# Fewer moving columns in the up products of experts with 129 to 224 tokens, in a fused attention and mixture-of-experts block

## The reference

```python
x = x + jnp.tanh(g_xattn[0]) * _L0_xattn_ref(_layernorm(x, axis=-1), ctx_512, ctx_512)
x = x + jnp.tanh(g_ffn[0]) * _L0_ffn_ref(_layernorm(x, axis=-1), L0_ffn_w_cls, L0_ffn_bias, L0_ffn_w_gate_up, L0_ffn_w_down)
```

```python
buf = jnp.zeros((E, CAP, H), xf.dtype).at[ids_s, pos].set(x_exp[order], mode='drop')
gu = jnp.einsum('ech,ehf->ecf', buf, w_gate_up)
g, u = jnp.split(gu, 2, axis=-1)
act = jax.nn.silu(g) * u
y = jnp.einsum('eci,eih->ech', act, w_down)
```

## Time and profile before

| | us |
|---|---|
| median of 3 runs | 2288.61 |
| lowest, highest | 2286.43, 2290.40 |
| the profiled execution, its own time | 2303.04 |
| its span, first to last instruction | 2301.2 |
| PE busy in the span | 2114.8 (92%) |
| DVE busy | 1453.7 (63%) |
| ACT busy | 1245.7 (54%) |
| POOL busy | 1072.1 (47%) |

### The profile page before, as it was taken

How to read it: one execution, slowest core, us unless ns; L and a number is a source line. 1 busy time by engine, 2 the same in 40 slices (tenths; PEclk the granted TensorE clock), 3 DMA queues, 4 the chain that set the end, 5 groups by cost and what they waited for, 6 DMA issues and landing times.

```text
span 2301.2 us, 48610 instructions
## 1 busy us (share of the span) xinstructions
PE 2114.8 (92%) x14776; PEld 1228.3 (53%) x14777; DVE 1453.7 (63%) x2463; ACT 1245.7 (54%) x1833; POOL 1072.1 (47%) x1241
## 2 busy tenths in 40 slices
PE   5999999989998596899999999999999999999996
PEld 2555554445554344456556564744656766454464
DVE  6788888888887564346446572833564865462383
ACT  3787777666775436235445463632553764353364
POOL 3127888877887465224322441622342643241262
PEclk9999999999999797999999999999999999999998
DMA  5567666657564656457666593955585986665582
GB/s 148 144 176 179 169 186 156 177 154 189 159 152 120 217 149 163 150 156 215 180 187 185 172 281 83 302 161 160 161 259 133 286 235 173 188 174 162 150 250 47
DMA packets 569277, 407.81 MB, mean 177 GB/s; under 512 B 213558, under 2 KB 489142, under 8 KB 569200
## 3 DMA queue, kind: packets, MB, share of 16 engines
q1 hardware_dynamic: 506112, 334.10, 50.1%
q0 software_dynamic: 46336, 72.10, 13.2%
q10 hardware_dynamic: 16752, 0.65, 0.5%
HBM read 319.33 MB, written 103.16 MB: 184 GB/s over the span
## 4 chain that ended last, share of the span: by engine, by line
PE 66%; DVE 14%; issue 9%; ACT 3%; POOL 3%; another core or an unknown queue 2%; DMA 1%; SPq 1%; DVEq 0%; POOLq 0%; ACTq 0%
PE psum L1673 35%; PE psum L1703 16%; DVE mx L1159 5%; PE psum L1560 5%; PE psum L1532 3%; PE psum L1545 2%; PE psum L1613 2%; DVE xgt L1328 1%; DVE stats L1124 1%; PE psum L1573 1%; DVE wgu L1316 1%; PE psum L1584 1%; DMA out_dram<-ys,slots 1%; PE psum L1509 1%
## 5 line engine op out<-in xcount | busy, mean ns | idle before, releaser
L1673 PE MATMUL psum<-xgt,wgu 128*128 128x256 f16 (+3 forms) x6336 | 907.0, 301 | 40.3 <-issue 25.1
L1673 PEld LDWEIGHTS psum<-xgt,wgu 128*128 (+1 forms) x6336 | 573.8, 98 | 372.7 <-issue 54.8
L807 POOL TENSOR_TENSOR spare<-spare 128x1 f32<-128x1 f32 x164 | 141.9, 865 | 856.1 <-PE psum L1703 432.5
L1703 PE MATMUL psum<-wdn,apair 128*128 128x512 f16 x1968 | 458.6, 384 | 19.1 <-issue 14.2
L1159 DVE TENSOR_REDUCE mx<-psum 128x2 f32<-128x512 f32 x512 | 327.3, 683 | 84.0 <-PE psum L1532 71.9
L1316 DVE SCALAR_TENSOR_TENSOR wgu<-wraw,wgu 128x1024 f16<-128x1024 f32 x264 | 318.4, 1216 | 41.2 <-ACT wgu L940 37.4
L724 POOL DMA_INDIRECT lists<-entry,dest x256 | 268.4, 1049 | 114.3 <-issue 69.7
L923 ACT ACTIVATE prob<-psum 128x512 f32<-128x512 f32 x512 | 277.3, 598 | 72.1 <-PE psum L1545 38.6
L1338 DVE SCALAR_TENSOR_TENSOR a<-psum,sg 128x512 f32<-128x512 f32 x132 | 91.0, 689 | 350.2 <-PE psum L1673 335.9
L1328 DVE COPY xgt<-psum 128x1024 f16<-128x1024 f16 x256 | 167.0, 682 | 225.0 <-PE psum L1613 206.4
L1703 PEld LDWEIGHTS psum<-wdn,apair 128*128 128x128 f16 x1968 | 187.9, 99 | 223.7 <-issue 30.4
(11 more groups left out here) (157 smaller groups left out, 1943.5 us busy)
## 6 DMA issues: line engine op xcount, KB each, us to landing
wraw<-in_L_ffn_w_gate_up_dram SPq DMA_DIRECT2D x264, 512.0 KB
wraw<-in_L_ffn_w_down_dram SPq DMA_DIRECT2D x132, 512.0 KB
x<-in_x_dram SPq DMA_DIRECT2D x16, 1024.0 KB
xr<-in_x_dram SPq DMA_DIRECT2D x16, 1024.0 KB
out_dram<-x SPq DMA_DIRECT2D x16, 1024.0 KB
pairs<-xs SPq DMA_DIRECT2D x16, 1024.0 KB
qs<-qh SPq DMA_DIRECT2D x248, 64.0 KB
qs<-ql SPq DMA_DIRECT2D x128, 64.0 KB
```

The source lines that it names most:

```text
L1673: mm = pe.matmul(ps_gu[:, s, h, 0:nt * P], w[:, a, k, :], xgt[:, c, k, 0:nt * P], start=(k == 0 and (a, c) == (0, 0)), stop=(k == KB - 1 a ...
L1703: mm = pe.matmul(psum[:, Y_BANK[i] + n2, :], apair[:, o, k, c * P:(c + 1) * P], w[:, a, k, :], start=(k == 0 and (a, o) == (0, 0)), stop=( ...
```

## The change

The width of the up products is taken from a table. It is unchanged for the arms 1, 3 and 4. In arm 2 the up products stream 224 columns where they streamed 256. The test that leads into arms 1 and 2 is now for at most 224 tokens where it was 256, so that an expert with 225 to 256 tokens goes into arm 3 (384 columns and three blocks). The down products, the transposes, and all that the other engines do are as they were. On TensorE no instruction is added, taken away or moved; the moving operand and the output of the 192 up matmuls of arm 2 are 32 columns narrower, and one constant of a comparison differs.

```diff
@@ -41,6 +41,7 @@
 TOPK = 8
 CAP = 512
 CT = CAP // P
+UP_COLUMNS = {1: P, 2: 7 * P // 4, 3: 3 * P, 4: CAP}
 FF = 512
 FB = FF // P
 ROUTE_SCALE = 1.5
@@ -1670,7 +1671,7 @@
                 pe.wait_ge(wgu_lo, 2 * n + h + 1)
                 for k in range(KB):
                     for a, c in TERMS:
-                        mm = pe.matmul(ps_gu[:, s, h, 0:nt * P], w[:, a, k, :], xgt[:, c, k, 0:nt * P],
+                        mm = pe.matmul(ps_gu[:, s, h, 0:UP_COLUMNS[nt]], w[:, a, k, :], xgt[:, c, k, 0:UP_COLUMNS[nt]],
                                        start=(k == 0 and (a, c) == (0, 0)), stop=(k == KB - 1 and a == 1))
                 mm.then_inc(gu_full, 1)
 
@@ -1774,7 +1775,7 @@
             def step2(e, last):
 
                 n = pe.value_load(filled[0:1, bass.ds(e, 1)], min_val=0, max_val=ntok)
-                with pe.If(n < 2 * P + 1):
+                with pe.If(n < UP_COLUMNS[2] + 1):
                     with pe.If(n < P + 1):
                         body(e, 1)
                     with pe.Else():
```

## The result

| | before | changed |
|---|---|---|
| median, us (4 runs each) | 2288.44 | 2264.49 |
| lowest, highest | 2286.43, 2290.40 | 2263.25, 2268.57 |
| the profiled execution | 2303.04 | 2268.57 |
| its span | 2301.2 | 2266.8 |

The ratio is 0.9902, with a 95% interval from 0.989 to 0.9914: 24.0 us faster, 1.0%. The forecast was 2268.3, or 20.3 us.

A forecast was written before the change was run, and what follows sets the result against it. TensorE was taken to bound the 33 steps; nine arm 2 steps of 2.19 us and one of 0.57 gave 20.3 us, taken off the median 2288.61 for 2268.3 us, range 2262 to 2275.

The forecast's parts named there:

- TensorE bounds the 33 steps: Whole step loop: TensorE's waits add up to 29 us over 1300 us, so a microsecond less there shortens the total.
- The price of 32 columns, 2.56 us a step: Up products of arm 2: 0.417 ns a column, 13.35 ns a matmul, 25.6 us over ten steps if nothing else holds TensorE.
- the one for paired loads: Skill's rule for matmuls each with its own weight load: 0.13 ns a column, winning only 8 us over 1920 up matmuls.
- The sequencer costs nothing at 224: Up products of arm 2: sequencer needs about 18.6 us against 18.40 streaming, covered by a lead of at least 1.4 us.
- A new wait of 0.37 us for `dn_lo(1)`: Before arm 2's first down matmul: low down weights on VectorE come late, so a step gains 2.19 us, not 2.56.
- The step from 1340.11 gains only 0.57: One arm 2 step where VectorE started late after a 1.85 us wait: down product at 20.39 us, gain only 0.57.
- the first rival: Start of arm 2's down products: the VectorE to TensorE latency hides, all 25.6 us come through, 2263.0 us; chance 0.12.
- The step from the profiled execution to the median: Whole kernel: profiled execution lies 14.4 us above the median; the 20.3 us are taken off the median, 2288.61.
- No expert changes arms: Branch into arm 2: its ten experts have at most 206 tokens, the nearest above 258, so the cost is nothing.
- the rival: Branch of `step2`: two or more experts fall into arm 3, a loss of 13.3 us and more, 2301.9; chance 0.03.

The follow-up runs named there:

- the split kernel: 224 columns as in the change, with the wait for the second low part of the down weights moved 9 down matmuls later; 2261.2 us, ratio 0.9884 to before.

## Why the prediction was right, and where not

- *TensorE bounds the 33 steps.* Right. What the steps of arm 2 lost on TensorE went out of the total, and no other engine came due, down to 192 columns.
- *The price of 32 columns, 2.56 us a step.* Right. The paces measured are 82.5 and 89.2 ns (192 and 208 columns, with the loop written out), 95.8 (224, from 18.40 us in the split kernel), 102.5 (240), 109.2 (256), 152.6 (360) and 162.6 (384), 0.417 ns a column throughout. The rule N/2.4 + 2.5 ns, which the prediction took from the Trainium skill (TensorE: Matmul & The Clock Gate, section Back-to-back issue gap), gives each of them to 0.1 ns; the one for paired loads does not hold here between 192 and 384 columns.
- *The sequencer costs nothing at 224.* Right, with less to spare than it looked: at 208 it costs 0.3 us inside the up products, and at 192, once the wait is split, all that the narrower width would bring.
- *A new wait of 0.37 us for `dn_lo(1)`.* Right in kind and place, and shown by taking it away. Its size was 0.27 to 0.31 us, since the way from VectorE to TensorE took 0.23 to 0.28 us in arm 2 and not the 0.34 read in arm 1. That row holds a different path, through `closing`, with a check or two more. Most of this way is not the signal: in the step shown, TensorE's check of `wdn_lo` (line 1712) begins 0.04 us after `dn_lo(1)` ends, and the other 0.2 us go by in register instructions and further checks before the first down matmul. Worth 0.7 us in all.
- *The step from 1340.11 gains only 0.57.* Wrong. The stop of 1.85 us on VectorE did not come again: that step gained 2.29 like the others. Nor did VectorE run "without a gap" after it; it stood still for 0.97 us ahead of `act_lo` of j=1, waiting for ScalarE. A stop seen once, from outside the engines, need not come again in its step. Worth 1.7 us.
- *The last step* gained 2.6 us rather than 2.19, because it does not wait for `dn_lo(1)` at all: its up products run 0.29 us over streaming in both traces, and `dn_lo(1)` is ready by then. Worth 0.4 us. With these three terms 20.3 becomes 23.1, and 24.0 were measured; the 0.9 between them is inside the interval.
- *The total.* That the stretch lost 20.3 us, the figure of the whole forecast, is chance: for its nine steps the forecast had 18.1 (eight of 2.19 and one of 0.57). By the total alone the first rival, no new wait and 2263.0 us, is nearer to the 2264.5 measured than the forecast's 2268.3. What decides for the forecast's mechanism is the trace, and the run with the split wait.
- *The step from the profiled execution to the median.* The 20.3 us were taken off the median, so that nothing hung on the 14.4 us by which the profiled execution was longer. That was the right way: for the changed kernel this excess was 4.1 us. That of before lay largely in steps 0 and 1 (132.8 us against 122.7), which vary.
- *No expert changes arms.* Right. The price of one, 15.4 us, left out the two transposes in `opening`; it is 16.7 against the 256 columns, 19.0 against the 224. With two such experts the kernel is slower than before, as the rival said, by 15.5 us where it gave 13.3.

## What to carry to other kernels

Where a matrix engine streams without idle time, its columns have a fixed price (here 0.417 ns each), and padding to a round number of blocks can be dropped to the width that the data need, as long as no group falls into the next wider arm. Before pricing it, look at the next thing to be late: here VectorE's low parts and TensorE's own sequencer stood within a microsecond of the up products. The first came just due at 240 columns, where `dn_lo(1)` ends the 0.28 us ahead that the way to TensorE takes; at 224 it took back about 0.3 of the 2.56 us. And read a variable kernel by the stretch that does not vary: steps 2 to 30 repeat to a tenth of a microsecond while whole executions scatter by several.

## What the runs showed of the hardware

- At 192 columns, with a weight load for each matmul and register arithmetic for the weights' address, the second half of the up products took 8.91 us for 96 matmuls, about 92 ns each. Inside each run of 24 it was 86 ns; the rest stood at the changes from one run to the next. With fixed addresses and the loop written out all 192 ran at 82.5 ns (15.84 us).
- From the end of a VectorE instruction to the matmul that waited for it passed 0.23 to 0.28 us where register instructions and further checks stood between (the steps in the loop). Where the wait stood on the weight load itself, in the last step of the changed kernel, that load began 0.05 us after the end (2244.62 after 2244.57), and it did so in the last step with 208 columns too.
- The profile's name for a wait on a line with several semaphores can be plainly wrong: 0.25 us were put down to `wdn` in a kernel where the part waited for had been ready for 4 us.
- Writing out a loop of two rounds, at 208 columns, made each of nine steps 0.6 to 0.8 us faster and cost about 8.5 us in two single stops, outside the code that was written out. The cause of the stops is not shown.
